# A selective-scan stage laid out anew: 32 channels by 4 states on the partitions, units of 512 positions in both directions, delta, du, b and c each spread by loads, drives on GpSimd

## What is computed

```python
def mamba(seq, p):                       # seq: [1024 sequences, 128 positions, 64 channels]
    x, z = split(einsum('blc,ec->ble', seq, in_w))           # 128 inner channels each
    x = silu(causal_conv(x, conv_w, conv_b))                 # 4 taps
    dt, Bm, Cm = split(einsum('bld,ed->ble', x, xp_w))       # 4, 16 and 16 values per position
    delta = softplus(dt @ dt_w + dt_b)                       # 128 channels
    A = -exp(A_log)                                          # 128 channels x 16 states
    # per position t, channel c, state n:
    #   h[c, n] = exp(delta[t, c] * A[c, n]) * h[c, n] + delta[t, c] * x[t, c] * Bm[t, n]
    #   y[t, c] = sum_n h[c, n] * Cm[t, n]
    return einsum('bld,cd->blc', (y + x * D) * silu(z), out_w)
```

## Time and profile before

| | |
|---|---|
| median of 3 executions | 40272.85 us (40259.12 to 40300.51) |
| the profiled execution | 40283.3 us, its span 40281.5 us |
| busy share: DVE, PE, POOL, ACT | 65%, 62%, 62%, 49% |
| granted TensorE clock, mean | 0.752 |
| moved by DMA | 7230 MB, 179 GB/s over the span |
| DMA queue's share of 16 engines | 75.6% |

### The profile page before, as it was taken

One profiled execution on the slowest core, in us unless ns is written; L12 is line 12 of the kernel. 1 busy time (PEld: TensorE's weight loads), 2 busy tenths in 40 slices (PEclk: granted clock), 3 DMA queues, 4 the chain that ended last, 5 costly groups with the idle time before them and its releaser, 6 DMA issues. The chain is left out here.

```text
span 40281.5 us, 323274 instructions
## 1 busy us (share of the span) xinstructions
PE 24925.9 (62%) x75932; PEld 7783.3 (19%) x75932; DVE 26249.4 (65%) x15920; ACT 19794.8 (49%) x25923; POOL 24988.5 (62%) x10756
## 2 busy tenths in 40 slices
PE   6666666666666666666666666666666666665384
PEld 1111111111111111111111111111111111111221
DVE  6666666666666666666666666666666666666211
ACT  5555555555555555555555555555555555554022
POOL 6666666666666666666666666666666666665000
PEclk7777777777777777777777777777777777777597
DMA  7777777777777777777777777777777777778767
GB/s 173 183 182 183 182 182 181 182 185 183 183 183 182 182 182 182 184 183 183 184 183 184 183 183 182 183 184 182 184 184 182 184 183 184 182 185 183 138 125 157
DMA packets 2491075, 7230.00 MB, mean 179 GB/s; under 512 B 444632, under 2 KB 708456, under 8 KB 2461672
## 3 DMA queue, kind: packets, MB, share of 16 engines
q1 hardware_dynamic: 2491000, 7229.05, 75.6%
HBM read 6086.95 MB, written 738.20 MB: 169 GB/s over the span
## 5 line engine op out<-in xcount | busy, mean ns | idle before, releaser
L781 POOL TENSOR_TENSOR read<-state,c_rep 128x1024 f32<-128x1024 f32 x8192 | 19168.1, 2356 | 11286.4 <-DVE state L718 11276.0
L595 ACT ACTIVATE decay<-decay,a_neg 128x1016 f32<-128x1016 f32 x5632 | 6436.3, 1143 | 15023.0 <-DMA decay<-delta_spread 15007.1
L718 DVE TENSOR_TENSOR_SCAN state<-decay,pair_ps 128x1024 f32<-128x1024 f32 x5632 | 12646.9, 2272 | 67.7
L703 DVE TENSOR_TENSOR pair_ps<-pair_ps,b_rep 128x1024 f32<-128x1024 f32 x5632 | 6723.3, 1223 | 8833.5 <-PE pair_ps L415 8829.8
L718 DVE TENSOR_TENSOR_SCAN state<-pair_ps,drive 128x1024 f32<-128x1024 f32 x2560 | 5835.3, 2279 | 1819.4 <-ACT pair_ps L598 1783.3
L765 POOL TENSOR_TENSOR drive<-drive,b_rep 128x1024 f32<-128x1024 f32 x2560 | 6016.7, 2350 | 844.7 <-DMA drive<-du_spread 844.7
L415 PE MATMUL pair_ps<-u_stack,spread 96*128 96x512 bf16 x11264 | 4035.5, 466 | 3314.9 <-DVE state L718 3287.4
L438 PE MATMUL y_bank<-read,sel_f 128*32 128x512 f32 x32768 | 4831.6, 716 | 33.2 <-POOL read L781 31.5
L381 PE MATMUL p_bank<-u,to_c 128*128 128x512 f32 x2048 | 1998.8, 1105 | 2818.7 <-ACT zs L527 2070.2
L595 ACT ACTIVATE pair_ps<-decay,a_neg 128x1016 f32<-128x1016 f32 x2560 | 2835.6, 1108 | 1361.3 <-DVE state L718 1361.2
L375 PE MATMUL p_bank<-xt,taps 128*128 128x512 f32 x4096 | 2489.2, 763 | 1042.5 <-DMA xt<-in_xs 1040.4
(11 more groups left out here) (105 smaller groups left out, 22317.9 us busy)
## 6 DMA issues: line engine op xcount, KB each, us to landing
decay<-delta_spread SPq DMA_DIRECT2D x8192, 512.0 KB, 5.2
drive<-du_spread SPq DMA_DIRECT2D x2560, 512.0 KB, 8.0
u_stack<-u_parts SPq DMA_DIRECT2D x6144, 64.0 KB, 10.2
delta_spread<-delta SPq DMA_DIRECT2D x512, 512.0 KB, 5.7
du_spread<-du SPq DMA_DIRECT2D x512, 512.0 KB, 4.2
xt<-in_xs SPq DMA_DIRECT2D x512, 256.0 KB, 14.2
rec<-o_sb SPq DMA_DIRECT2D x512, 128.0 KB, 5.8
c_img<-x SPq DMA_DIRECT2D x16, 4096.0 KB, 50.5
```

Of the source, the lines that this page charges most:

```text
L595: ins = nc.scalar.activation(inner(dst, d), inner(src, d), ACT.Exp, scale=a_neg[s][:, 4 * j + k:4 * j + k + 1])
L703: nc.vector.tensor_tensor(ps, ps, b_rep[d][:, :], ALU.mult).then_inc(s_drive_v, 1)
L718: nc.vector.tensor_tensor_scan(state[:, q % H_RING, ::step], a, x, 0.0, ALU.mult, ALU.add).then_inc(s_state, 1)
L781: nc.gpsimd.tensor_tensor(read[:, q % R_RING, :], state[:, q % H_RING, :], c_rep[d][:, :], ALU.mult).then_inc(s_read, 1)
```

## The change

The scan stage is written anew; the stages behind it stay.

- A unit is now half a tile, 4 sequences (512 positions), in both directions. The columns of a 1024-wide tensor are FWD first and then REV. There are still 512 units of 16 pairs.
- The 128 partitions of a pair hold 32 channels by 4 states. Pair `q` is row `m` of 4 states and block `j` of 32 channels, `m, j = divmod(q, 4)`.
- Four loads each of 128 x 1024 spread delta (`delta_rep`), du (`du_rep`), b (`b_rep`) and c (`c_rep`), 16 loads in a unit, where there were 16 of delta and 5 of du. b and c are stored to DRAM as well (`bc_spread`), from one projection of 32 rows per direction.
- The three bf16 parts of du, `u_stack`, the spread matmuls and their take-offs are gone, and so is the ring of `decay` tiles in SBUF. `decay` is now two tiles in PSUM, written by ACT (L541) from `delta_rep`.
- All 16 drives are made by POOL (L728) from `du_rep` and `b_rep`, up to three pairs ahead.
- A scan is two instructions of 512 columns, one per direction (L664). For 11 pairs it writes to `state_ps` in PSUM and DVE makes the reads (L676, two of 512); for the 5 pairs of `BY_POOL` it writes to SBUF and POOL makes the read (L737).
- There is one `p_bank` of 512 columns instead of two, and one `y_bank`; the steps stand in the table `STEPS`.

```diff
-PAIRS = 16
-BY_POOL = (2, 5, 8, 11, 14)
+PAIRS, ROW = 16, 4
+WIDE = 2 * HALF
+USEQS = SEQS // 2
+BY_POOL = (1, 4, 7, 10, 13)
-D_RING, H_RING, R_RING = 4, 4, 8
+DRIVE_RING, READ_RING, STATE_RING = 4, 8, 2
+DRIVE_AHEAD = 3
...
+STEPS = [Step("dt", REV, 1, 0, 0), Step("bc", 0, 1, 1, 1), Step("ds", FWD, 1, 4, 5),
+         Step("ds", REV, 1, 6, 7), Step("out", 0, -1, 8, 9), Step("x", FWD, 2, 11, 12),
+         Step("x", REV, 2, 12, 13), Step("z", 0, 1, 13, 14), Step("dt", FWD, 2, 14, 15)]
...
-            def load_drive(d, g):
-                sp.dma_start(drive[:, g, :], group_rows(spill["du"][d], BY_POOL[g])
-                             ).then_inc(s_dug[g], 16)
+            def store_bc(h, d):
+                sp.dma_start(spill["bc"][h][:, px(d)], bc[32 * d:32 * d + 32, :]).then_inc(s_bc, 16)
+            def store_delta(h, taken):
+                sp.wait_ge(s_evac, taken)
+                sp.dma_start(spill["du"][h], e_log[:, :]).then_inc(s_spill, 16)
+                sp.dma_start(spill["delta"][h], e_one[:, :]).then_inc(s_spill, 16)
+            def channels(dram, j):
+                return bass.AP(dram.tensor, dram.offset + 32 * j * WIDE,
+                               [[0, 4], [WIDE, 32], [1, WIDE]])
+            def states(dram, m):
+                return bass.AP(dram.tensor, dram.offset + 4 * m * WIDE,
+                               [[WIDE, 4], [0, 32], [1, WIDE]])
+            def load_delta(h, j):
+                sp.dma_start(delta_rep[:, j, :], channels(spill["delta"][h], j)).then_inc(s_delta[j], 16)
+            def load_du(h):
+                for j in range(ROW):
+                    sp.dma_start(du_rep[h][:, j, :], channels(spill["du"][h], j)).then_inc(s_du[h][j], 16)
+            def load_b(h, m):
+                sp.dma_start(b_rep[:, m, :], states(spill["bc"][h][0:NS, :], m)).then_inc(s_b[m], 16)
+            def load_c(h, m):
+                sp.dma_start(c_rep[:, m, :], states(spill["bc"][h][NS:2 * NS, :], m)).then_inc(s_c[m], 16)
...
+                    at_least(sp, s_ysum, ROW * U)
+                    load_c(h, 3)
+                        load_x(i + 1, h)
+                        sp.wait_ge(s_evac, taken["bc", 0])
+                        store_bc(1 - h, FWD)
+                        sp.wait_ge(s_drive, PAIRS * U + 4)
+                        store_bc(1 - h, REV)
+                        sp.wait_ge(s_bc, 32 * (U + 2))
+                        load_b(1 - h, 0)
+                        sp.wait_ge(s_ysum, ROW * U + 1)
+                        load_c(1 - h, 0)
+                        sp.wait_ge(s_drive, PAIRS * U + 8)
+                        load_b(1 - h, 1)
+                        store_delta(1 - h, taken["ds", REV])
                         sp.wait_ge(s_spill, 32 * (U + 2))
-                        for g in range(3):
-                            load_drive(1 - d, g)
+                        load_du(1 - h)
+                        sp.wait_ge(s_ysum, ROW * U + 2)
+                        load_c(1 - h, 1)
+                        sp.wait_ge(s_drive, PAIRS * U + 12)
+                        load_b(1 - h, 2)
+                        for j in range(2):
+                            sp.wait_ge(s_decay, PAIRS * U + 13 + j)
+                            load_delta(1 - h, j)
...
-                nc.vector.tensor_tensor_scan(state[:, q % H_RING, ::step], a, x, 0.0,
-                                             ALU.mult, ALU.add).then_inc(s_state, 1)
+                    out = state_ps[:, :]
+                for d in range(2):
+                    step = 1 if d == FWD else -1
+                    nc.vector.tensor_tensor_scan(out[:, px(d)][:, ::step],
+                                                 decay[q % 2][:, px(d)][:, ::step],
+                                                 drive[:, q % DRIVE_RING, px(d)][:, ::step], 0.0,
+                                                 ALU.mult, ALU.add).then_inc(s_state, 1)
+            def read_state(U, q):
+                m, j = group_of(q)
+                dve.wait_ge(s_c[m], 16 * (U + 1))
+                for d in range(2):
+                    dve.wait_ge(s_state, 2 * PAIRS * U + 2 * q + d + 1)
+                    nc.vector.tensor_tensor(read[:, q % READ_RING, px(d)], state_ps[:, px(d)],
+                                            c_rep[:, m, px(d)], ALU.mult).then_inc(s_read_v, 1)
...
+                nc.gpsimd.tensor_tensor(drive[:, q % DRIVE_RING, :], du_rep[h][:, j, :],
+                                        b_rep[:, m, :], ALU.mult).then_inc(s_drive, 1)
```

More of the change, by code:

```diff
@@ L150, in scan_stage @@
[L150 to L162, removed]
@@ new lines, in scan_stage @@
+        bc = sb("bc", [2 * 32, HALF])
+        e_abs = sb("e_abs", [P, WIDE])
+        e_one = sb("e_one", [P, WIDE])
+        e_log = sb("e_log", [P, WIDE])
+        vpos = sb("vpos", [P, WIDE])
+        gated = sb("gated", [P, HALF])
+        o_sb = sb("o_sb", [CH, HALF])
+        delta_rep = sb("delta_rep", [P, ROW, WIDE])
+        du_rep = [sb(f"du_rep{h}", [P, ROW, WIDE]) for h in range(2)]
+        b_rep = sb("b_rep", [P, ROW, WIDE])
+        c_rep = sb("c_rep", [P, ROW, WIDE])
+        drive = sb("drive", [P, DRIVE_RING, WIDE])
@@ L170, in scan_stage @@
+        state = sb("state", [P, STATE_RING, WIDE])
+        read = sb("read", [P, READ_RING, WIDE])
+        decay = [pb(f"decay{n}", [P, WIDE]) for n in range(2)]
+        state_ps = pb("state_ps", [P, WIDE])
+        y_bank = pb("y_bank", [P, HALF])
+        p_bank = pb("p_bank", [P, HALF])
         s_load = sem("weights_loaded")
@@ L283, in spill_du @@
[L283 to L293 removed]
+                x = x[:, USEQS * h:USEQS * h + USEQS, :]
@@ new lines, in body @@
+                        if q == GATE and not (prev is None and h == 0):
+                            z_taken = FIRST_TAKEN - 1 + TAKEN * (U - 1)
+                            gate(U - 1, 1 - h, z_taken, before_unit(i, h, nxt, "out")[0])
+                        for s, _, before, _ in numbered(i, h, nxt):
+                            if s.kind == "ds" and DU[s.d] == q:
+                                make_du(1 - h, s.d, before + 1)
+            def tail(i):
+                rows = numbered(i - 1, 0, None)
+                z_taken = [after for s, _, _, after in rows if s.kind == "z"][0]
+                gate(2 * i - 1, 1, z_taken, numbered(i - 1, 1, None)[-1][1])
@@ L769, in body @@
+            for q in range(DRIVE_AHEAD):
+                make_drive(0, 0, 0, q)
             def body(i, prev, cur, nxt):
-                for U, d, w_next, pairs in units(i, cur, nxt):
-                    start, steps = steps_before(i, d), plan(d, w_next is not None)
-                    number = {(s.kind, s.half): start + n + 1 for n, s in enumerate(steps)}
-                    taken = start if d == REV or prev is None else start - len(OUT)
+                for U, h, w_prev, w_next, w_next2 in units(i, prev, cur, nxt):
```

776 lines of the change are left out of this document (329 added, 447 removed).

## The result

The changed kernel takes 51093.47 us (median of 4, 51066.91 to 51113.28) for 40265.99 us of the kernel before on the same chip (median of 4, 40191.47 to 40300.51): 1.2692 times as long, 95% interval 1.267 to 1.2714. The profiled execution has a span of 51087.4 us.

What follows compares the result with a forecast made beforehand. DMA was taken as the bound, before and after: loads 144 us, other transfers 6.7 and round trips 5 make 155.7 us a unit; 512 units are 79.7 ms, plus 3.16 and some 0.1: 83.0 ms. Range 60 to 90 ms.

Steps and rivals of the forecast that it cites:

- Four engines serve the loads: Scan-stage loads of delta, du, b and c: outermost source count 4 puts each on the same four DMA engines; given 0.82.
- both sides must divide: DMA loads: the engine count, up to 16, must divide the outer steps of both source and destination, giving 4 here.
- rival A: Scan-stage loads: all sixteen engines serve them, DVE bounds, 60 us a unit, 33.9 ms, 16% faster; chance 0.13.
- C: Scan-stage loads: an outside zero stride is not counted, so only b and c loads are confined; 55.2 ms, chance 0.03.
- the sign: Whole kernel: slower than before at 0.86, faster at 0.13, same at 0.01.
- The load on four engines: Each 524288-byte load in the scan stage takes 9.0 us at 14.6 GB/s an engine; sixteen take 144 us a unit.
- rival B: Scan-stage loads: four engines, each faster with twelve idle; 5.7 us a load, 103 us a unit, 55.9 ms; chance 0.10.
- Stores, small transfers and round trips: Scan-stage unit: spills 4.5 us, x, bc and rec 2.2 us, two round trips 5 us, together 11.7 us.
- DVE and POOL: Scan-stage compute: DVE 55.9 us a unit, perhaps 52, POOL 49 us, both hidden beside the loads.
- D: Scans through PSUM take 2.3 us a half, DVE 80 us a unit, 44 ms, showing only with sixteen engines; chance 0.02.
- The point of no gain: Scan-stage loads: at 3.8 us a load, below 9.5 engines' worth, the kernel becomes slower than before.
- Signs to look for: Scan-stage profile if right: landings well above 9 us, DMA share near 0.27, about 64 GB/s, DVE busy near 35%.

Runs made afterwards that it cites:

- e1: The changed kernel with partitions reordered so the source patterns of its loads have outermost count 32 instead of 4: 33080.06 us, ratio 0.8217 to the kernel before.
- e2: The changed kernel, partition order kept, each load issued as four DMAs of 32 partitions with outermost count 32: 33373.22 us, ratio 0.8289 to the kernel before.
- b1: The kernel before with decay and drive loads turned to outermost count 8 instead of 16, and w_keys loaded as 32 and 8 rows: 53470.66 us, ratio 1.328.
- b2: The kernel before with decay and drive loads reading 32 outer steps of 4 channels for 16 of 8, computing other values: 37164.29 us, ratio 0.9232.
- e4: e1 with its delta and du loads reading 16 outer steps of 8 channels, computing other values: 33369.99 us, ratio 0.8289 to the kernel before.
- e5: e1 with each load issued as two DMAs of 64 neighbouring partitions, 16 outer steps of 4 each: 33420.6 us, ratio 0.8302 to the kernel before.
- e8: e1 with each load issued as four DMAs of 32 neighbouring partitions, 8 outer steps of 4 each: 36442.01 us, ratio 0.9044 to the kernel before.
- e7: e1 with the two du products on DVE one pair later: 30702.57 us, ratio 0.7623 to the kernel before.
- e6: The changed kernel with only the four delta loads of a unit issued as four DMAs of 32 partitions each: 48274.1 us, ratio 1.1992 to the kernel before.

## Why the prediction was right and wrong

- **Four engines serve the loads: right.** Share 0.25 in load stretches, and 32 outer steps give sixteen (e1, e2). Also right is that both sides must divide: with 128 partitions as the destination, the share followed the source's count, 0.25 for 4, 0.52 for 8 (b1), 1.02 for 32 (e1). With it stand rival A's refusal, C's (both kinds of load were confined), and the sign.
- **The load on four engines: the step that failed.** It was sized at 9.0 us, from 14.6 GB/s as a rate of each engine, and measured 5.1. Sixteen of them were to take 144 us of a unit and take 81; with that one number put right the sum gives 81 + 11.7 = 93 us, against 93.6 measured, and 51 ms.
- **Why the rate was wrong.** 14.6 was a limit of the loads before, not of an engine. It lies on the destination's side and goes with the block of partitions that a step or a DMA fills (b2, e4, e2, e5, e8); that two engines meet there on the way into SBUF is the inference above. The four engines of the change run at 26, as the sixteen of e1 do (415 / 16). That `w_keys` showed 14.4 on ten engines looked like a second witness; the other runs say that it was none, and what held those loads is not settled (40 neighbouring partitions are a narrow destination too). The row that spoke against it was in the prediction itself, 369 GB/s or 23 an engine; it was kept as a bound and in rival B, at 0.10. B was the right rival: its 5.7 us is the nearest price to the 5.1 measured, though sixteen engines reach 26 GB/s as well, so idle neighbours are not what makes the four fast. C's 55.2 ms lies nearer to the time, but by chance, since both kinds of load were confined. The prediction also misread what moved there, so that its bound came from a store and loads together. The timeline of the kernel before shows that the stack copies were issued only behind that window; the store of delta and two decay loads filled it:

```profile
20064.75 0.49 SPq L281 DMA_DIRECT2D delta_spread<-delta  x1
20066.87 2.70 SPq L271 DMA_DIRECT2D decay<-delta_spread  x2
20071.93 0.33 SPq L285 DMA_DIRECT2D du_spread<-du  x1
20072.31 2.69 SPq L290 DMA_DIRECT2D u_stack<-u_parts  x4
```

- **Stores, small transfers and round trips: right as a sum**, 11.7 us against 93.6 - 81 = 12. Not every part was: the stores were put at 234 GB/s and ran at 383, so the agreement is in part luck.
- **DVE and POOL: right.** A half scan takes 1.213 us (1.21 forecast), PSUM to PSUM too, so D is out; a half read 0.673 (0.69); POOL 2.35. Of the two sums for a unit, 55.9 us and "perhaps 52", the second is right: DVE is busy 95% of e7's unit of 53.8 us, which is 51.3.
- **Rival A, worked out for sixteen engines: near.** It gave 60 us and 33.9 ms; e2, whose loads have the 234 GB/s that A assumed, has 59.0 and 33.4.
- **The point of no gain: a little too high.** It was put at 3.8 us a load. Units of 65.0 us at 2.8 (e8) and 93.6 at 5.1 (after), joined by a line, cross 72.5 at 3.4.
- **Signs to look for:** the share of 0.27 came (0.28); 64 GB/s did not (106); with that share, about 95 was named as the mark of B or C. DVE is busy 53%, not 35%, which follows from the shorter unit.

Left open: why the four engines of the changed kernel do not meet. By the map of the Trainium skill (SBUF — State Buffer, the same section) partitions 0 to 31 and 32 to 63 have the same ports. If these are two engines' blocks, they should meet, and yet each engine moves 26 GB/s. They may run out of step with each other, and the 84 and 86 GB/s of e6 and of the changed kernel may be stretches in step; no run tried it. Nor is it explained why each of b1's eight engines moves 16 GB/s, neither 14.6 nor 26.

## What to carry to other kernels

Read a hand-built access pattern of a DMA twice: its outermost count decides how many engines serve it (4 gave a share of 0.25), and how many neighbouring partitions each step fills can decide their rate (16 steps of 8 gave 234 GB/s, 32 steps of 4 gave 415). A rate per engine taken from a full burst is not a property of the engine until a burst on fewer engines, or another destination, shows the same. When a large change loses, run it once with only the layout of its transfers put right: here that turned 51.1 ms into 33.1, and showed the next bound.

## What was not expected of the hardware

- Share 1.02 with 234 GB/s looked like a full DMA. It was not: the share counts the time in which packets are under way, also when they take longer. The same sixteen engines moved 415 GB/s at the same share (e1). By an estimate from these rows, 4096 bytes took 16 * 1.02 * 4096 / 234 = 286 ns in the one case and 161 ns in the other.
- The kernel before could have run its loads faster: with 32 outer steps it took 37.2 ms for 40.3 (b2). So 3.1 of the 7.2 ms between it and e1 are the loads' rate, if that part carries over.
- 32 or 64 neighbouring partitions as a destination have little more than half the rate of 128: 234 and 238 GB/s against 415 (e2, e5, e1).
